# Layer 2's experts issued by chunks inside the stage of layers 0 to 2

## What is computed

```
layer 0: s = Mamba-like mixer (rotated q, causal conv, state-space scan)  f = gated MLP with weights and inputs rounded to 4 bits
layer 1: s = attention between the 16 heads of a token, 1.5-entmax         f = 8 experts of width 256, the best 2 of a token
layer 2: s = xn + out_w(gated groupnorm(readout(recurrence)))              f = 8 experts of width 176, the best 2, and a shared one
layer 3: s = causal attention with relative positions, 16 heads            f = gated MLP with int8 weights
```

## Time and profile before

| | us |
|---|---|
| median of 3 runs | 3222.31 (3211.36 to 3226.47) |
| the profiled execution | 3217.52 |
| its span, first to last instruction | 3215.7 |
| `layers012` after the set-up | 157 to 1971 |
| `outputs2` | 1971 to 2261 |
| `layer3` | 2261 to 3216 |
| busy in the span: DVE, PE, ACT | 2548.0, 2390.4, 1665.8 |

### The profile page before, as it was taken

The page is one execution under the profiler, slowest core; times in us unless marked ns, Lnnn a source line. Parts: engine busy times, 40 slices in busy tenths (PEclk is TensorE's granted clock), DMA queues, the critical chain, the costliest instruction groups (busy, mean ns, idle before and its releaser), DMA issues.

```text
span 3215.7 us, 39978 instructions
## 1 busy us (share of the span) xinstructions
PE 2390.4 (74%) x13590; PEld 1307.3 (41%) x13729; DVE 2548.0 (79%) x5554; ACT 1665.8 (52%) x3215; POOL 560.1 (17%) x610
## 2 busy tenths in 40 slices
PE   3688686867858858667767311899689898898988
PEld 1334233333334333333332110333266676676763
DVE  3396798898998999989989765778578787777874
ACT  1335444436236254443452322566578887788872
POOL 0000300300301103003021020000333233232320
PEclk9788797878977969878878555899799999999999
DMA  2001010101001100000011003210488878888751
GB/s 68 1 15 46 10 42 31 28 22 38 25 22 43 31 28 24 22 31 22 25 34 36 10 24 91 66 33 1 154 245 240 225 227 231 220 233 224 231 165 43
DMA packets 270757, 265.92 MB, mean 83 GB/s; under 512 B 15224, under 2 KB 244234, under 8 KB 268986
## 3 DMA queue, kind: packets, MB, share of 16 engines
q1 hardware_dynamic: 270554, 263.37, 28.7%
HBM read 130.48 MB, written 124.45 MB: 79 GB/s over the span
## 4 chain that ended last, share of the span: by engine, by line
PE 42%; DVE 33%; ACT 11%; issue 8%; DMA 2%; POOL 2%; SPq 1%; DVEq 0%; POOLq 0%; ACTq 0%
PE banks L2642 6%; PE banks L2688 3%; PE banks L2602 2%; ACT t L2629 2%; PE banks L422 2%; DVE t L955 2%; DVE t L1020 2%; PE banks L1085 2%; PE banks L1089 2%; ACT t L2553 2%; DVE t L952 1%; DVE t L1017 1%; DVE t L1169 1%; PE banks L2215 1%; PE banks L2544 1%
## 5 line engine op out<-in xcount | busy, mean ns | idle before, releaser
L2618 DVE CUSTOM_DVE_ANT_0 t<-banks,t 128x640 f32<-128x640 f32 (+7 forms) x512 | 379.8, 752 | 96.1 <-PE banks L2642 33.3
L2629 ACT ACTIVATE t<-t 128x640 f32<-128x640 f32 (+7 forms) x512 | 390.3, 780 | 55.0 <-DVE t L2618 53.5
L2642 PE MATMUL banks<-ident,t 128*128 128x128 f32 x2304 | 363.5, 283 | 43.1 <-ACT t L2629 23.6
L2642 PEld LDWEIGHTS banks<-ident,t 128*128 128x128 f32 x2304 | 253.2, 142 | 118.2 <-ACT t L2629 52.4
L1119 ACT ACTIVATE t<-banks 128x512 f32<-128x512 f32 x128 | 76.5, 598 | 299.1 <-PE banks L1085 298.7
L548 POOL TENSOR_TENSOR t<-t 128x512 f32<-128x512 f32 x28 | 48.1, 1717 | 983.7 <-ACT t L520 983.7
L2583 POOL TENSOR_TENSOR t<-t 128x512 f32<-128x512 f32 x96 | 122.7, 1278 | 530.8 <-DMA t<-relative_scratch 496.4
L1740 ACT ACTIVATE t<-t 128x16 f32<-128x16 f32 x256 | 82.8, 324 | 253.8 <-DVE t L1704 201.2
L2673 DVE COPY t<-banks 128x512 f32<-128x512 f32 x256 | 176.2, 688 | 36.4 <-PE banks L2642 32.6
L2602 PE MATMUL banks<-t 128*128 128x512 bf16 (+3 forms) x640 | 173.5, 323 | 16.0 <-DVE t L2618 8.9
L1085 PE MATMUL banks<-t 128*128 128x512 f32 x256 | 144.6, 648 | 32.6 <-DVE t L1165 31.7
(11 more groups left out here) (453 smaller groups left out, 5996.8 us busy)
## 6 DMA issues: line engine op xcount, KB each, us to landing
relative_scratch<-t SPq DMA_DIRECT2D x128, 512.0 KB, 3.5
t<-relative_scratch SPq DMA_DIRECT2D x128, 512.0 KB, 5.1
relative_scratch<-t SPq DMA_DIRECT2D x128, 256.0 KB, 4.1
t<-in_wmoe SPq DMA_DIRECT2D x64, 384.0 KB, 3.1
t<-cut_scratch SPq DMA_DIRECT2D x192, 64.0 KB
t<-t SPq DMA_DIRECT2D x16, 512.0 KB, 4.6
cut_scratch<-t SPq DMA_DIRECT2D x8, 768.0 KB, 4.1
z_scratch<-t SPq DMA_DIRECT2D x8, 512.0 KB, 3.3
```

Source lines behind the costliest of these rows:

```text
L2618: nc.vector.tensor_tensor_reduce(s.s[z][:, 0:n], ps[:, b0:b0 + 1 + i // 4, :].rearrange("p b n -> p (b n)")[:, 0:n], s.bias[r][:, j, WIDE ...
L2629: nc.scalar.activation(s.s[z][:, 0:n], s.s[z][:, 0:n], ACT.Exp, scale=-1.0, bias=s.least[:, z:z + 1]).then_inc(*a.mark("weights", u))
L2642: nc.tensor.transpose(ps[:, 4 + c % 2, (t - lo) * P:(t - lo + 1) * P], s.s[u % NS][:, t * P:(t + 1) * P], k.ident[:]).then_inc(*e.mark("tu ...
```

## The change

1. The experts of layer 2 move into `layers012`. `moe2_pe/act/dve(k, s, u)` now do one unit of 512 columns (a chunk of all batches); even units are part `n` (half0, banks 0 to 2, the mixer's), odd units part `o` (half1, banks 5 to 7, those of layer 1's experts). `n` may start when the mixer's last unit is done, `o` when layer 1's is, since they use memory that these leave (`outputs2_views`). Each unit keeps its silu output in `s.gate[u]`.
2. Readout (`p`) follows the last recurrence unit in the same weave, in bank S0 and the next; it now also does `out_w` and the sum into `s.s_T`. The last unit's retrieved values go from PSUM straight into `o.ret`.
3. The product with silu and the sum with x become part `z` (`ends2_dve`), 8 times two instructions, last of all.
4. The weights and scratch loads are turns `l` of SP's order; the meeting and the block of loads between the stages go. `xT` is allocated first and holds K and Q of the recurrence until then.
5. All orders of `layers012` are new, for the old parts too; from unit 3 to unit 7 DVE's repeats a string of 358 turns, but for a few letters. The work of the old parts is the same, instruction for instruction.

```diff
-def moe2_pe(k, s, half, b):
+def moe2_pe(k, s, u):
...
+    pe.wait_ge(k.queue("o2_loads"), "all")
+    pe.wait_ge(k.queue(f"xn_back{u}"), "all")
+    if again:
+        pe.wait_ge(v, "scaled", u - 2, E2 - 1)
+    elif half:
+        pe.wait_ge(k.line("att1_dve"), "x", LAST)
+    else:
+        pe.wait_ge(k.line("mixer_dve"), "x", LAST)
...
 def back_act(k, s, u, o):
+    out = o.ret[:, :, u * P:(u + 1) * P] if u == UNITS0 - 1 else s.ret_f
...
+def ends2_dve(k, s, u):
+    nc, dve, v, g = k.nc, k.dve, k.line("ends2_dve"), by_batch(s.gate[u])
+    tt, xt = nc.vector.tensor_tensor, of_unit(k.xT[:], u)
+    yield
+    dve.wait_ge(k.line(f"moe2{u % 2}_act"), "gate", u)
+    dve.wait_ge(k.line("out2_dve"), "summed", B - 1, 1)
+    tt(g, g, of_unit(s.s_T, u), ALU.mult).then_inc(*v.mark())
+    yield
+    dve.wait_ge(v)
+    dve.wait_ge(k.queue("x1_back"), "all")
+    tt(xt, xt, g, ALU.add).then_inc(*v.mark("x", u))
...
 def outputs2_sp(k, s, keep):
+    yield
+    k.sp.wait_ge(k.line("mixer_dve"), "x", LAST)
+    sp.dma_start(s.f_up, d["up2"]).then_inc(*loads.mark())
...
+    yield
+    k.sp.wait_ge(k.line("rec_dve"), "ret", LAST)
+    for b in range(B):
+        sp.dma_start(chunks(s.s_T[:, b * T:(b + 1) * T]), of_batch(keep.xn, b)).then_inc(*k.queue(f"s_T_back{b}").mark("all"))
+    yield
+    for n in range(RINGX):
+        k.sp.wait_ge(k.queue(f"x1_stored{n}"), LAST - (LAST - n) % RINGX)
+    sp.dma_start(k.xT[:], keep.x1).then_inc(*k.queue("x1_back").mark("all"))
+    for b in range(1, B):
+        yield
+        k.sp.wait_ge(v, "y", b - 1)
+        zx_back(b)
...
  def readout2_pe(k, s, b):
...
+    for h in range(2):
+        yield
+        pe.wait_ge(v, "y", b)
+        pe.wait_ge(a, "root", b)
+        for j in range(2):
+            mm(bank(ps, S0 + h), s.out_w[:, j], s.y[:, j, h * TB:(h + 1) * TB], start=(j == 0), stop=(j == 1)).then_inc(*e.mark("out", b, h))
...
     layers012(k, keep)
-    k.xT = nc.alloc_sbuf_tensor("xT", [P, B * T], F32)
-    with ExitStack() as held:
-        outputs2(k, held, keep)
```

More of the change, by code:

```diff
@@ L41 @@
 ATT1, WORK, MOE1 = 6784, 5464, 5 * TB + 140
+MIXER, HEADS, EXPERTS, STRAND = 12496, 7168, 5772, 4224
 class Line:
@@ L1816 @@
[L1816 to L1820, removed]
@@ L1927, in every, with units2, side_by_side_pe @@
     return straight(*(part(u) for u in range(UNITS0)))
-def side_by_side_pe(k, s):
+def units2(part, half):
+    return straight(*(part(u) for u in range(half, UNITS0, 2)))
+def side_by_side_pe(k, s, o):
     free = banks_free(k)
@@ L2008, in layers012 @@
         s.at = s.coef[:].rearrange("p n a j -> p n (a j)")
-        s.rows, s.kd = sb([P, NBL, BS, DH2 + 1]), sb([P, NBL, BS, DH2])
+        strand = sb([P, STRAND])
+        take = carved(strand)
+        s.rows = take((NBL, BS * (DH2 + 1))).rearrange("p n (l d) -> p n l d", l=BS)
+        s.kd = take((NBL, BS * DH2)).rearrange("p n (l d) -> p n l d", l=BS)
+        o = outputs2_views(s, mixer, heads, experts, work, strand)
         early = carved(work)
@@ L2092, in outputs2_read_sp, with xn_back, zx_back @@
-def outputs2_read_sp(k, s, keep):
-    sp, v = k.nc.sync, k.line("out2_dve")
-    z, xc = k.queue("z_back"), k.queue("xconv_back")
-    for b in range(B):
-        if b:
-            k.sp.wait_ge(v, "y", b - 1)
+    z, xc, v = k.queue("z_back"), k.queue("xconv_back"), k.line("out2_dve")
+    def xn_back(u):
+        k.sp.wait_ge(k.queue("xn_stored"), u)
+        sp.dma_start(s.xn[u], unit(keep.xn, u)).then_inc(*k.queue(f"xn_back{u}").mark("all"))
+    def zx_back(b):
         for j in range(2):
@@ new lines, in outputs2_sp @@
+    sp.dma_start(s.f_down[0:F2S[0], 0], d["down2"][0:P]).then_inc(*loads.mark())
+    sp.dma_start(s.f_down[0:F2S[1], 1], d["down2"][P:F2]).then_inc(*loads.mark())
+    xn_back(0)
+    yield
+    for out, name in ((s.wr, "wr2"), (s.sup, "sup2"), (s.half[0].rb.lower, "c_lower")):
+        sp.dma_start(out, d[name]).then_inc(*loads.mark())
+    sp.dma_start(s.ebias, d["eb2"].unsqueeze(0).partition_broadcast(P)).then_inc(*loads.mark())
+    yield
+    sp.dma_start(s.sdown[0:F2S[0], 0], d["sdown2"][0:P, :]).then_inc(*loads.mark())
@@ new lines, in outputs2_sp @@
+    sp.dma_start(s.sdown[0:F2S[1], 1], d["sdown2"][P:F2, :]).then_inc(*loads.mark())
+    sp.dma_start(s.f_pick[0:3 * E2], d["c_pick"]).then_inc(*loads.mark("all"))
+    xn_back(2)
+    yield
+    reads = k.queue("o2_reads")
+    for out, name in ((s.read_w, "readw2"), (s.group, "c_group"), (s.gn_w, "gnw2"), (s.gn_b, "gnb2"), (s.dp, "dp2")):
+        sp.dma_start(out, d[name]).then_inc(*reads.mark())
+    sp.dma_start(s.out_w, d["outw2"].rearrange("(k p) n -> p k n", p=P)).then_inc(*reads.mark("all"))
@@ new lines, in outputs2_sp @@
+    yield
+    k.sp.wait_ge(k.line("att1_dve"), "x", LAST)
+    sp.dma_start(s.half[1].rb.lower, d["c_lower"]).then_inc(*k.queue("o2_lower").mark("all"))
+    for u in (1, 3, 4, 6):
+        xn_back(u)
+    yield
+    k.sp.wait_ge(k.queue("z_stored"), LAST)
+    k.sp.wait_ge(k.queue("xconv_stored"), LAST)
+    zx_back(0)
+    yield
+    k.sp.wait_ge(k.line("in2_dve"), "kq", LAST)
+    k.sp.wait_ge(k.line("turn2_act"), LAST, 1, 3)
+    xn_back(5)
+    xn_back(7)
+    yield
+    k.sp.wait_ge(k.queue("ret_stored"), LAST - 1)
@@ L2228, in moe2_pe @@
+    for t in range(NT):
+        mm(ps[:, bb, t * E2:(t + 1) * E2], xn[:, t * P:(t + 1) * P], s.wr, start=True, stop=True).then_inc(*e.mark("logits", u))
+    yield
+    if again:
+        pe.wait_ge(a, "hid", u - 2, E2 - 1, 1)
+    mm(bank(ps, bc), s.sup[:, 0:P], xn, start=True, stop=True).then_inc(*e.mark("shared", u, 0))
+    yield
+    pe.wait_ge(v, "comb", u)
     for t in range(NT):
-        mm(ps[:, bb, t * E2:(t + 1) * E2], xn[:, t * P:(t + 1) * P], s.wr[:], start=True, stop=True).then_inc(*e.mark("logits", b))
+        nc.tensor.transpose(ps[0:E2, bb, t * P:(t + 1) * P], o.rb.comb[:, t], k.ident[:]).then_inc(*e.mark("comb", u))
```

529 lines of the change are left out of this document (271 added, 258 removed).

## The result

The changed kernel takes 3111.6 us (median of 4 executions, 3101.6 to 3117.7) where the kernel before took 3217.2 beside it: ratio 0.9666, 95% interval 0.9627 to 0.9705. It is faster, 8 us under the forecast of 3120, and inside the range. Measured twice more beside its variants, it came out at 0.9655 (0.9635 to 0.9675) and 0.9645 (0.9624 to 0.9666).

What follows compares the result with a forecast made beforehand. DVE was taken to bound the full weave, a chain of waits the end. Gains of 91.8 (filling and tail) and 10 (order), 102 in all, take 3217.5 to 3115.5; with 4.8 for the median, 3120 us, range 3080 to 3190.

Steps and rivals of the forecast that it cites:

- Term 3: Steady stretch of layers 0 to 2: the new order of the old parts gains 10 us, bounds +79 to -79.
- The feared loss: Units 2 to 7: a string planned with wrong durations errs every period; 20 us a unit gives 3240; 7 in 100.
- The table's 35 loads: ScalarE in the new order: the table is asked for 35 times less (125 to 90), each load 1.28 us.
- Term 1: Mixer's end to recurrence's end: layer 2's experts as filler, 0.48 us of DVE a turn; "ret" of unit 7 at 2052.7.
- DVE over 0.88 busy: Sign of being right: some 250 us between layer 1's last sum and "ret" with DVE this busy.
- Term 2: Behind the recurrence: turning back, four readouts of 24 us, ends of 11 us and 6 us extra take 117 us.
- The ceiling of 152: Upper bound of the tail: each of 14 hops a batch meets a whole 0.69 us filler.
- Here the chain sets the time: Tail: DVE has only about 36 + 36 + 11 us of work in 117, so the serial readouts decide its length.
- The covers: Side checks that PE's clock rises so DVE still bounds, and that SP's queued loads cost nothing.
- the rival of a badly packed tail: Filled stretches and tail: PE stays at the slow clock, fillers arrive late; gain 21 to 55, about 3185; 15 in 100.
- POOL's turns of unit 7: Last unit's angle turns beside fuller DVE: nearer 33 than 24 us, up to 9 us more; 5 in 100 as deciding.
- SP's new waits: SP's load order: first load turns wait for the mixer's last unit, with a K copy and expert loads behind; costed at nothing.

Runs made afterwards that it cites:

- experiment 1: Kernel before with only the new order of layers 0 to 2, output stage and memory as before: 3183.3 us, ratio 0.9898 to the kernel before.
- experiment 2: Changed kernel with expert chunk turns between the mixer's last turn and the recurrence's end moved behind it: 3235.2 us, ratio 1.0051 to the kernel before.
- experiment 5: Changed kernel without the readouts' variance steps (squares, sum, small product, root, reciprocal): 3106.4 us, ratio 0.9658 to the kernel before.
- experiment 6: experiment 4's kernel with only the turns behind the recurrence in a newly planned order: 3098.1 us, ratio 0.9632 to the kernel before.
- experiment 7: experiment 4's kernel plus a second y buffer, two readouts in flight, turns replanned: 3104.4 us, ratio 0.9646 to the kernel before; run again, 0.9625.
- experiment 4: Changed kernel with final gating by batch behind each readout, only chunks 6 and 7 at the end: 3105.1 us, ratio 0.9641 to the kernel before.

## Why the prediction was right, and where its sums were off

**Two sizes were off and cancelled.** The order was put at 10 us and is worth 34; the chunks with all that goes with them were put at 92 and are worth 3183.3 - 3111.6 = 72 in medians (83 in the spans). 106 in all, 102 forecast. Each lay inside the bounds that the prediction gave; that the sum came within 4 us of the forecast gain is luck.

**Term 3, the order, is the step that failed in size.** It looked only at the one wait that the new string visibly answered (11.3 us in the earlier trace rows). That wait did fall, to 3.5 us, which is 8 of the 34. Another 9.9 us came from the stretch ahead of the first recurrence, which the prediction did not look at. The rest is spread over other waits, some of which fell as far (line 1541, 8.3 us, gone from the weave) while others grew (line 1141, to 11.3). In experiment 1's trace layer 1's last sum is 26.6 us sooner, 9.9 ahead of the first recurrence and 16.7 behind it; the 10 us of the prediction were meant for the latter alone. So in the changed kernel that sum came at 1772.3 instead of near 1793. The feared loss, a wrongly planned string that errs in every period, did not happen: the recurrences of units 1 to 5 end 216 us apart, before 219. The table's 35 loads were counted right (127, now 92).

**Term 1, the fill.** Without chunks layer 1's last sum comes at 1762.4 (experiment 1) or 1759.3 (experiment 2), with them at 1772.3: 10 to 13 us where 14.2 were added, all of DVE's idle time having been called used. From there to the recurrence's end: 120.1 us to the gates (forecast 110, ceiling 133.3) and 136.1 to the end (139.5), 256.2 against 249.5. Here too two errors lean against each other: DVE had 215.9 us of work where 230.0 were priced, and stood idle 40.3 us where 19.5 were. The step that was too hopeful is DVE's share in the first part: it was 0.79 busy, not 0.921. The waits of DVE in both parts show who was late:

```profile
DVE t L1346 <- ACT t L1306: 9.8, 4, 3.2
DVE t L2514 <- ACT t L2460: 7.0, 10, 1.8
DVE t L2510 <- ACT t L2455: 5.8, 8, 1.6
DVE t L2477 <- PE banks L2370: 3.8, 7, 1.1
```

The first row, the squares of the earlier trace rows, still costs 9.8 us (was 16.3), and the experts' answers from ACT come to 13 us. So "DVE over 0.88 busy" held for the second part (0.886) and not for both (0.843).

**Term 2, the tail.** 122.0 us against 117. Readouts 25 us apart against 24; the ends 10.7 against 11. (The ceiling of 152 adds up to 150 from its own terms.) The number was right and its reason only half: experiment 5 shows that a shorter chain alone changes nothing, experiment 6 that one other order alone does not either, and experiment 7 that both together bring the readouts to 16 to 22 us. The chain of waits and the written order lay close to each other, and once both are changed, as experiment 7 shows, the last experts end 5 us behind the last readout's sum. "Here the chain sets the time" is thus not true of the chain alone.

**What experiment 2 adds.** The prediction priced experts by DVE's turns, 0.48 us each. In the gaps of the chain they cost less than that (94 us for 252 turns, 0.37 each); by themselves, in these turns, the experts cost twice what they cost as filler. As filler they brought DVE some 106 us of work (11 up to layer 1's last sum, 95 behind it) and made the recurrence end 94 later, so the chain's gaps swallowed only about 12 us of their work. The change pays because the experts are taken out of a place where they pack badly, more than because a place with room was found. This is a reading of the traces; no experiment separates the two.

**The covers.** TensorE's clock was 0.83 and 0.77 in the filled stretches (forecast: above 0.7), so the rival of a badly packed tail at the slow clock fell. DVE did not wait for POOL's angles at all (forecast: under 5 us; 12.9 before), since fillers stand in front. POOL's turns of unit 7 took 29.2 us, between the 23.9 and 33.2 of the earlier trace rows, nearer the latter as said. Their timeline, and DVE's beside it:

```profile
1902.67 0.45 POOL L1609 TENSOR_TENSOR t<-t 128x126 f32<-128x126 f32 x1
...
1903.34 2.76 POOL L1604 TENSOR_TENSOR t<-t 128x248 f32<-128x248 f32 x1
1906.06 2.70 POOL L1605 TENSOR_TENSOR t<-t 128x248 f32<-128x248 f32 x1
```
```profile
1903.30 2.28 DVE L1655 TENSOR_TENSOR t<-xT,t 128x2048 f32<-128x2048 f32 x1
1905.51 2.74 DVE L1657 TENSOR_TENSOR t<-xT,t 128x2048 f32<-128x2048 f32 x1
```

Two POOL products of 248 columns take 2.7 us; one of 252 at 1900.96 took 0.61. Each begins beside one wide DVE product and ends 0.5 us behind it, and the second DVE product takes 2.74 us instead of 2.28. By the Trainium skill ("SBUF — State Buffer", section "SBUF: two separate sides") a DVE instruction with two SBUF inputs and a GpSimd instruction that reads SBUF share a port pair, and the one that starts first holds it for its whole instruction while the other blocks. The trace agrees: DVE's first product began at 1903.30, POOL's at 1903.34. SP's new waits cost nothing that shows.

## What to carry to other kernels

Price a filler by what it costs where it now stands, not only by the busiest engine's share of it: the same experts, in the same order, cost 4.5 us each alone and 2.0 in gaps. Where a new order of a steady stretch comes with a change, look at all the idle time of its bounding engine, the start included, and not only at the wait that one can see answered. Behind a written order a shorter chain can be worth nothing until the order is written again, as here, and once both are mended look for the next chain close behind. Take apart what a variant carries: of the 12 us of experiment 7 about half were experiment 4's.

## What the runs showed beyond that

- **The same turns end at different times.** Eight profiled kernels have the same turns up to the recurrence's end; its last sum began between 2014.2 and 2033.6 us. Little of it comes from the full weave: from the first "ret" to the mixer's last unit all eight take 1068.3 to 1071.2 us. Layer 3, untouched, took 953.4 to 966.6 us. The 5.9 us that it lost in the changed kernel's first trace lie within that, and gains of 5 to 10 us, as in experiments 4 and 7, drown in it.
- **In one kernel the whole time goes with TensorE's mean granted clock, in another it does not.** The six executions of the kernel of experiment 6 ran from 3117.5 us at 0.865 to 3089.9 at 0.875; two of experiment 7's ran 3089.1 and 3103.1 us, both at 0.868. What moves the time was not tested.
- **A table load costs all or little of its 1.28 us** by where it stands: about 1.25 us ahead of the first recurrence, 0.3 in the full weave.
